# Summing a group's last tiles row by row in two graph layers, with each row's sum inverted and scaled by itself

## The reference, cut to what matters

```python
# layer 1
h = relu(layernorm(x))
a = (adj == 1);  deg = a.sum(axis=1)
x = x + ((a @ h) / deg) @ W.T + b
# layer 2
h = relu(layernorm(x)) @ W
e = leaky(h @ a[:D] + (h @ a[D:]).T, slope=0.01)
att = softmax(where(adj > 0, e, -1e12), axis=1)
x = x + elu(att @ h)
```

## Time and profile before

| | us |
|---|---|
| median of 3 runs | 2406.94 (2406.09 to 2406.97) |
| profiled execution, its own time | 2404.54 |
| its span, first to last instruction | 2402.9 |
| layer 1 (first cast to the last group's inversions) | 936 to 1203 |
| layer 2 (first `p32` to the last group's inversions) | 1230 to 1675 |
| TensorE, VectorE, ScalarE busy over the span | 93%, 75%, 57% |

### The profile page before, as it was taken

The page is one execution under the profiler, slowest core; times in us unless marked ns, Lnnn a source line. Parts: engine busy times, 40 slices in busy tenths (PEclk is TensorE's granted clock), DMA queues, the critical chain, the costliest instruction groups (busy, mean ns, idle before and its releaser), DMA issues. The chain is left out here.

```text
span 2402.9 us, 45799 instructions
## 1 busy us (share of the span) xinstructions
PE 2239.1 (93%) x17180; PEld 1701.0 (71%) x17180; DVE 1810.4 (75%) x2893; ACT 1370.8 (57%) x2132; POOL 111.3 (5%) x124
## 2 busy tenths in 40 slices
PE   5899999999999998999978999988899999999998
PEld 4677777767677676888867777777356666666667
DVE  6967778697887954121169999998598998898896
ACT  6655465555646556666555555454355565665556
POOL 2000000010100100000000000000000000000000
PEclk9899999999999999999989999999899999999999
DMA  7543241423401112222211222221211111111010
GB/s 176 108 67 47 52 80 40 80 45 71 82 30 45 45 54 93 88 83 87 70 45 58 66 69 67 74 65 39 88 36 36 44 49 46 30 53 54 23 32 27
DMA packets 62934, 146.72 MB, mean 61 GB/s; under 512 B 10023, under 2 KB 14778, under 8 KB 61757
## 3 DMA queue, kind: packets, MB, share of 16 engines
q1 hardware_dynamic: 56461, 110.57, 14.9%
q0 software_dynamic: 5760, 33.56, 8.4%
q10 hardware_dynamic: 560, 0.52, 0.1%
HBM read 170.30 MB, written 41.43 MB: 88 GB/s over the span
## 5 line engine op out<-in xcount | busy, mean ns | idle before, releaser
L2101 PE MATMUL bank<-VB,ph 128*128 128x257 f16 x1936 | 492.6, 278 | 54.1 <-ACT ag L2002 21.4
L2102 PE MATMUL bank<-VB,ph 128*128 128x257 f16 x1936 | 491.3, 277 | 0.0
L192 PE MATMUL bank<-s_row,kT_hi 128*128 128x512 f16 x1024 | 306.1, 381 | 8.2 <-DMA s_row<-qT_d 6.3
L1558 PE MATMUL bank<-VA,ph 128*128 128x257 f16 x1024 | 281.1, 274 | 7.9 <-DVE VA L1167 7.9
L2105 PE MATMUL bank<-VB,pl 128*128 128x257 f16 x1024 | 286.5, 280 | 0.0
L2733 PE MATMUL bank<-VA,w_dense 128*128 128x257 f16 x1024 | 281.0, 274 | 3.0 <-ACT w_dense L2594 2.4
L1560 PE MATMUL bank<-VA,pl 128*128 128x257 f16 x1024 | 280.9, 274 | 0.0
L1559 PE MATMUL bank<-VA,ph 128*128 128x257 f16 x1024 | 280.9, 274 | 0.0
L2735 PE MATMUL bank<-VA,pl 128*128 128x257 f16 x1024 | 280.6, 274 | 0.0
L2734 PE MATMUL bank<-VA,w_dense 128*128 128x257 f16 x1024 | 280.6, 274 | 0.0
L2101 PEld LDWEIGHTS bank<-VB,ph 128*128 128x128 f16 x1936 | 190.8, 99 | 95.5 <-ACT ag L2002 30.6
(11 more groups left out here) (338 smaller groups left out, 4538.3 us busy)
## 6 DMA issues: line engine op xcount, KB each, us to landing
mask<-mask_d SPq DMA_DIRECT2D x256, 256.0 KB, 2.7
mask_d<-in_adj POOLq DMA_DIRECT2D x8, 2048.0 KB, 23.4
xg<-x SPq DMA_DIRECT2D x16, 512.0 KB, 4.2
x<-xo POOLq DMA_DIRECT2D x16, 512.0 KB, 2.9
xg<-in_x SPq DMA_DIRECT2D x8, 512.0 KB, 12.5
x<-xg SPq DMA_DIRECT2D x8, 512.0 KB, 3.9
qT_d<-qTg POOLq DMA_DIRECT2D x8, 512.0 KB, 2.9
s_row<-qT_d SPq DMA_DIRECT2D x8, 512.0 KB, 4.3
```

Source lines behind the costliest of these rows:

```text
L192: last = nc.tensor.matmul(out_ap, st, mv, start=(i == 0), stop=(i == len(todo) - 1))
L1558: nc.tensor.matmul(acc, ph[:, u % HR, c], v_row(V, 0, t), start=(t == 0), stop=False)
L2101: nc.tensor.matmul(acc, p_hi, v_at(V, 0, t), start=first, stop=False)
L2102: last = nc.tensor.matmul(acc, p_hi, v_at(V, 1, t), start=False, stop=final and not weighted)
```

## The change

In each group's last quad, TensorE goes row by row: it waits until all four tiles are there, then puts all four into bank 0, then bank 1, and so on. After rows 0, 1 and 2 it raises a new semaphore, `pe_r`; row 3's products raise `pe_q` for the four tiles, so that their buffers are given back in the last quarter of the quad. In layer 1 each group's first quad goes by rows too. The inversions become `inverse(g, i0, i1)`, each of which waits for its own row. In layer 1 they stand where they stood. In layer 2 rows 0 to 2 are inverted after quad (g, 0)'s four `p32`, ahead of its `pl`, and row 3 after the second `pl`; for the last group they stay in part 0. ScalarE's scalings already waited for each row's inversion, and their code and place are unchanged. The number of products, inversions, scalings and DMAs is the same.

```diff
-        def aggregate(V, side, slope=None, wh=None, sums_first=False):
+        def aggregate(V, side, slope=None, wh=None):
...
-                        if q == 0 and not isinstance(g, int) and sums_first:
-                            denominators(g - 1)
+                        if q == 0 and not isinstance(g, int):
+                            inverse(g - 1, 0, R - 1)
                         for r in range(R):
+                            if r == 2 and q == 0 and not isinstance(g, int):
+                                inverse(g - 1, R - 1, R)
                             dve.wait_ge(act_q.sem, act_q.at(n, "hi", r))
...
-                    def denominators(g):
-                        dve.wait_ge(pe_q.sem, pe_q.at(g * Q + (Q - 1), "pv", R - 1))
-
-                        dve.wait_ge(act_s.sem, act_s.before(g, "ag", R - 1))
-                        for r in range(R):
-                            nc.vector.reciprocal(rden[:, r:r + 1], bank[r][:, D:D + 1]
-                                                 ).then_inc(dve_s.sem, dve_s.one("rden", r))
+                    def inverse(g, i0, i1):
+                        for i in range(i0, i1):
+                            if i < R - 1:
+                                dve.wait_ge(pe_r.sem, pe_r.at(g, "row", i))
+                            else:
+                                dve.wait_ge(pe_q.sem, pe_q.at(g * Q + (Q - 1), "pv", R - 1))
+                            if i == 0:
+
+                                dve.wait_ge(act_s.sem, act_s.before(g, "ag", R - 1))
+                            nc.vector.reciprocal(rden[:, i:i + 1], bank[i][:, D:D + 1]
+                                                 ).then_inc(dve_s.sem, dve_s.one("rden", i))
 
                     def part(dve, g, q):
-                        if q == 0 and (not sums_first or isinstance(g, int)):
-                            denominators(g)
+                        if q == 0 and (isinstance(g, int) or not weighted):
+                            inverse(g, 0, R)
                         work["dve"](dve, g, q)
...
+                    def quad_by_rows(g, q):
+                        for r in range(R):
+                            made(g, q, r)
+                        for i in range(R):
+                            if q == 0:
+                                pe.wait_ge(act_s.sem, act_s.before(g, "ag", i))
+                            for r in range(R):
+                                last = tile_row(q, r, i)
+                                if i == R - 1:
+                                    last.then_inc(pe_q.sem, pe_q.one("pv", r))
+                            if q == Q - 1 and i < R - 1:
+                                last.then_inc(pe_r.sem, pe_r.one("row", i))
+
                     def quad(g, q):
-                        n = g * Q + q
+                        if q == Q - 1 or (q == 0 and not weighted):
+                            return quad_by_rows(g, q)
                         for r in range(R):
...
+                            made(g, q, r)
                             for i in range(R):
-                                if first:
+                                if q == 0 and r == 0:
                                     pe.wait_ge(act_s.sem, act_s.before(g, "ag", i))
...
+                                last = tile_row(q, r, i)
                             last.then_inc(pe_q.sem, pe_q.one("pv", r))
```

More of the change, by code:

```diff
@@ L141, in build @@
         pe_q, act_q, dve_q = (Steps(sem(n)) for n in ("pe_quad_done", "act_quad_done", "dve_quad_done"))
-        steps = (pe_s, act_s, dve_s, pool_s, pe_q, act_q, dve_q)
+        pe_r = Steps(sem("pe_row_summed"))
+        steps = (pe_s, act_s, dve_s, pool_s, pe_q, act_q, dve_q, pe_r)
         s_xin = sem("x_loaded")
@@ L1910, in aggregate @@
                 pe_q.plan(("pv", R))
+                pe_r.plan(("row", R - 1))
                 act_q.plan(("hi", R))
@@ L2081, in _, with made @@
                 def _(pe):
+                    def made(g, q, r):
+                        n = g * Q + q
+                        if weighted:
+                            pe.wait_ge(dve_q.sem, dve_q.at(n, "lo", r))
+                            if isinstance(g, int):
+                                pe.wait_ge(v_lo.sem, v_lo.upto(q * R + r))
+                                if q * R + r == 0:
+                                    pe.wait_ge(v_col.sem, v_col.upto(1))
+                        else:
+                            pe.wait_ge(act_q.sem, act_q.at(n, "hi", r))
@@ new lines, in tile_row @@
+                    def tile_row(q, r, i):
+                        t = q * R + r
+                        first, final = t == 0, t == T - 1
+                        acc = bank[i][:, 0:D + 1]
+                        c = slice(i * P, (i + 1) * P)
+                        p_hi = ph[:, slot(q, r), c]
+                        nc.tensor.matmul(acc, p_hi, v_at(V, 0, t), start=first, stop=False)
+                        last = nc.tensor.matmul(acc, p_hi, v_at(V, 1, t), start=False, stop=final and not weighted)
+                        if weighted:
+                            last = nc.tensor.matmul(acc, pl[:, slot(q, r), c], v_at(V, 0, t), start=False, stop=final)
+                        return last
@@ L2132, in aggregate @@
             loaded[0] += G * Q // MS
-            for x_ in (pe_s, act_s, dve_s, pool_s):
+            for x_ in (pe_s, act_s, dve_s, pool_s, pe_r):
                 x_.close(G)
```

## The result

The changed kernel takes 2413.24 us (median of 11 runs, 2411.67 to 2415.14) against 2406.78 for the kernel before (11 runs, 2404.84 to 2409.29). The ratio is 1.0025 with a 95% interval of 1.0016 to 1.0034: slower by 6.5 us, where 6.1 were forecast. The profiled execution took 2413.80 us with a span of 2412.1, 9.2 above the span of before.

The account below looks back on a forecast made before the run. It took TensorE's pauses to bound layer 1 and a VectorE-TensorE loop layer 2. Layer 1's -6.3 and layer 2's +12.4 gave +6.1, so 2410.6 us profiled; with 2.4 for the median, 2413.0, range 2408 to 2419.

Parts of the forecast that it names:

- Layer 1, later boundaries: Six boundaries between groups: scalings start earlier and the stutter goes, saving 0.96 us each, 5.8 us in all.
- Layer 1, group 0: TensorE must wait for all four casts, against the boundary loss saved: +0.6 us, between -0.2 and +1.4.
- Layer 1, tail, Layer 2, tail: After the last group only row 3's scaling is left uncovered: -1.1 us at most.
- Layer 2, group 0: Quad 7 starts some 1.2 us later, after the fourth `VB` tile, so VectorE waits for rows: +1.4 us.
- Layer 2, VectorE in the later groups: Six later boundaries: VectorE waits for nothing worth naming; three more semaphore waits cost 0.3 us in all, bounds 0 and 2.3.
- Layer 2, quad 2: TensorE's pause grows to 5.9 us and the clock falls, 2.1 us at 7 restarts: +11.8 us net, bounds 6.2 and 17.4.
- Layer 2 together: Sum of that layer's terms, 1.4 + 0.3 + 11.8 - 1.1: +12.4 us.
- a clock that holds at quad 2: Rival for layer 2: no half clock behind the longer pause, so faster, 2398.3 us; chance 0.15.
- restarts that are all as cheap as the cheapest: Rival for layer 2's quad 2: the clock falls but each restart costs the least seen, 2407.4 us; chance 0.17.
- VectorE does wait for rows: Rival for layer 2: row sums seen 0.5 us later delay `pl` in 6 groups, +3, 2416 us; chance 0.10.
- ScalarE does hold layer 1: Forecast's assumption; the rival, ScalarE not holding it, gave 9.6 us gained in place of 5.8, 2409.2 us; chance 0.08.

Follow-up runs that it names:

- the old pause put back: The changed kernel, but in layer 2 all inversions again stand behind quad 0's four `pl`, TensorE still going by rows: 2399.35 us, ratio 0.9967.

## Why the prediction was right

It named one mechanism for layer 2, half clock behind a longer pause at quad 2, and the runs show that one: filling the pause gives the time back, and so does restoring the older one. By its own steps, from the two profiled executions:

- *Layer 1, later boundaries.* 0.96 us each forecast, 37.23 - 36.23 = 1.00 measured: 6.0 for 5.8. ScalarE's casts are what limits it, as said: the scalings start right behind them, and TensorE still waits 0.45 us, for 0.6 forecast.
- *Layer 1, group 0.* +0.6 forecast, +1.3 measured, near the top of its bounds. From the first cast to the last product of group 1 it is 981.57 - 937.48 = 44.09 us, and was 979.09 - 936.26 = 42.83. Quad 7 starts 2.3 us behind the first cast where it was 0.7, and its products are at the spacing of half clock for 5.5 us (939.80 to 945.34), 2.6 before.
- *Layer 1, tail.* From the last product to layer 2's first `p32` it is 26.91 us for 27.94: -1.0 for -1.1.
- *Layer 1 together*, first cast to layer 2's first `p32`: 288.43 us against 294.16, so -5.7 where -6.3 was forecast.
- *Layer 2, group 0.* This term was mis-sized: +1.4 forecast, +2.6 measured, as `p32` of quad 1 in group 1 now begins 7.97 us behind that of quad 0 (1280.59 to 1288.56) and began 5.34 behind it (1285.10 to 1290.44). I had quad 7 starting late but at full clock. It starts at 1280.26 behind a pause of 2.66 us, where the pause ahead of quad 7 had been 1.47, and at half clock; rows 1 and 2 come late by it, and VectorE waits 1.18 and 1.16 us for them:

```profile
1280.20:1283.40 3.20, 3.14 (x15) 2.25 (x16) 2.98 (x7) 1.86 (x3) 0.00 (x0) 0.51 0.07 24
```

- *Layer 2, VectorE in the later groups.* +0.3 forecast, nothing measured: the period of the second group is 57.18 us, 2.48 more than before, and its quad 2 alone took 2.49 more. Three inversions in a row stand without a wait.
- *Layer 2, quad 2.* The pause was 5.99 to 6.20 us for 5.9. The seven restarts cost 1.71, 2.49, 2.89, 1.44, 2.35, 2.83 and 1.40 us, each being its 48 products' time less 5.19: together 15.1 where 7 x 2.1 = 14.7 was forecast, and less the 2.9 of before 12.2 for 11.8. All lie within the 1.3 to 2.9 taken from the rows.
- *Layer 2, tail.* The last product now precedes the ELU's first step by 1685.81 - 1684.79 = 1.02 us, before by 2.17; -1.15 for -1.1.
- *Layer 2 together*, first `p32` to VectorE's first step of layer 3: 488.13 us against 474.32, +13.8 where +12.4 was forecast; the 1.4 is group 0's 1.2 and the restarts' 0.4, less the 0.3 of the later groups.

The profiled pair differs by 9.2 us, 1.2 of which is already there at layer 1's first cast, ahead of all that was changed; the medians differ by 6.5. That the forecast meets them to half a us is partly luck. By the stages both layers came out worse than forecast, by 0.6 and by 1.4 us, 8.1 in place of 6.1, and the profiled execution took 2413.80 us for 2410.6. The forecast then added 2.4 us, by which the profiled execution of before lay under its median; that of the changed kernel lies 0.6 above its own.

Of the rivals, a clock that holds at quad 2 is out for this kernel, and so are restarts that are all as cheap as the cheapest, though two of the seven were (1.44 and 1.40 us). VectorE does wait for rows, but at the first boundary alone. ScalarE does hold layer 1.

The rule of the Trainium skill that the prediction weighed (TensorE: Matmul & The Clock Gate, "Why this matters for your kernels", no pause above some 3 us) agrees with the pauses of 6 us, all seven of which were followed by half clock. The runs differ from it on both sides: behind four waits of 3.5 us, in the changed kernel with 20 products, the clock was full, and behind one pause of 2.66 us, in the changed kernel, it was not.

## What to carry to other kernels

Find the loop of waits that makes the period before removing a pause: if the engine waits again a little later for something that doesn't move, the pause is only added to that one. On TensorE this can be worse than useless: here one pause of 6 us at the head of its critical stretch lowered the clock on the stretch that counts in seven of seven groups, where the two of 2.3 and 2.5 us before it had cost nothing on the loop in six of seven. Where such a pause can't be avoided, products without use that end before the awaited data comes can keep the clock up: the 48 here ended some 0.5 us ahead of it, and 20, which left 3.5 us, were enough in four groups of seven.

## What was unexpected of the hardware

Pauses of the same length had different outcomes. Behind waits of 3.5 to 3.7 us at quad 2 the clock was full in four groups and low in three. Pauses of 2.3 us at the boundaries of layer 2 lowered it in six groups of the kernel before (not at the first, where the pause was 2.13; the prediction's "each of the groups" was one too many). In that kernel with 20 products, a first pause of 2.14 us lowered it as well. The same pauses of 2.3 us left it full in one group of six with rows in layer 1 alone, and in two of six with 20 products besides. Pauses of 2.5 us at quad 2 lowered it in none, in six groups of the kernel before and in six with the old pause put back. What else decides was not tried.
